# Expert rows stored as fp16 halves, a quarter of the experts transposed by the DMA crossbar, down matrices stored by partition

## The chip, the cores and the metric

One core of a Trainium2 chip runs the whole program. The metric is device time in microseconds (us) of one execution; lower is better. Engines are named as in the profile: PE (TensorE matmul), PEld (its weight loads), DVE (VectorE), ACT (ScalarE), POOL (GpSimd), SP (SyncE, which here only issues transfers).

## The reference

One post-layernorm decoder layer on x of 16 sequences x 256 rows x 512 columns (4096 rows in all), float32:

```python
x = layernorm(x + self_attention(x))          # 3 heads of width 512, averaged, then fc_w
x = layernorm(x + cross_attention(x, ctx))    # 16 heads of 32, causal
x = layernorm(x + ffn(x))
# ffn: router over 64 experts, top 6 of each row, at most 128 rows per expert
buf = rows of x gathered per expert                       # (64, 128, 512)
g = silu(einsum('ech,ehf->ecf', buf, w_gate))             # F = 352
u = einsum('ech,ehf->ecf', buf, w_up)
d = einsum('ecf,efh->ech', g * u, w_down)
y = sum over the row's 6 experts of weight * d
y = y + (silu(x @ sh_gate.T) * (x @ sh_up.T)) @ sh_down.T # shared expert, width 704
```

## The kernel before

Every matrix product is done in fp16 with each float32 operand split into a high half and a low half (x = high + low); three products high*high, high*low, low*high are summed (`PASSES`). Splitting takes one ACT copy (the high half) and one DVE subtraction (the low half).

The program has three stages. `prepare` folds weights (to about 71 us). `attend` loops over the 16 sequences in 18 software-pipelined bodies (to about 1290 us); it ends each sequence with the second layernorm's rows `x2`. `experts` runs the 64 experts, with jobs of the shared expert in between (to about 1940 us), and then normalizes and stores.

**End of a sequence in `attend`.** ACT (ZH, L1164) writes the high half of x2 to `x2r`, DVE (ZL, L1307) the low half. SP (L847) stores x2 as float32 rows to `x2_d` (for the gathers) and to `moe_d` (the sums), then waits for the halves and issues two crossbar transposes (L852) of `x2r` to `x2s`, each 128 x 1024 fp16, waits for them, and stores `x2s` to `x2T_d` (L855). The router's product on PE reads `x2s`.

**Experts.** `all_jobs` writes one list `MOE` of steps, and every engine walks it in this order, doing its own part. The steps of turn e are: G(e) gate product; HT(e-1) transposes of the hidden rows; U(e) up product; X(e+1) transposes of the next expert's gathered rows; WG(e+1) weight split; one to three jobs of the shared expert; WU(e+1); D(e-1) down product; WD(e). PE jobs use 8 PSUM banks in a ring. A step X(e) is four float32 128x128 transposes on PE (L1766) against an identity, with stride 4 through the row, so that chunk c holds columns 4q+c; then ACT (L1854) writes the high half and DVE (L1948) the low half of `xgs`. POOL gathers the rows of expert e (L1665, 128 rows of 2 KB) into one of three slots of `xg`; the slot is free once X(e-3) is done on PE. POOL also adds each expert's output to `moe_d` (L1680), one add at a time, in the order of the list.

**SP in the experts.** After each weight split is done on DVE (semaphore `w_low`), SP issues the load of the same matrix for expert e+3: L144 for gate or up (704 KB, one transfer, 5632 bytes per partition), L151 and L154 for down (512 and 192 KB, runs of 2 KB). All go through one hardware queue, as do the crossbar transposes.

## Time and profile before

| | |
|---|---|
| median of 3 runs | 2048.06 us (2028.49 to 2049.26) |
| the profiled execution's own time | 2014.67 us |
| its span, first to last instruction | 2012.9 us |
| granted TensorE clock, mean | 0.993 |
| PE busy | 1953.1 us (97%) |
| DVE, ACT, POOL busy | 1667.5, 1021.5, 692.8 us |
| DMA packets, MB | 202021, 285.59 |

The span is what the instructions cover; the time of the execution adds 1.8 us around it. The three timed runs lie 14 to 35 us above the profiled one. Busy shares are averages over stages: what bounds the kernel is read stage by stage. In a row of the timeline the first number is the start in us from the span's start and the second the duration; for queues (SPq) it is the time in which the instruction was issued, and the transfer's landing comes later.

### The profile page before, as it was taken

Reading aid. Unit: us, or ns where it says so; the run is one execution under the profiler, and the core shown is the slowest. Engines: PE = TensorE matmul, PEld = TensorE weight load, DVE = VectorE, ACT = ScalarE, POOL = GpSimd, SP = SyncE. Lnnn points to the kernel's source line nnn. Section 1 sums busy time; section 2 is a strip of 40 time slices with the busy share of each in tenths; the row PEclk is TensorE's granted clock in tenths of the full one; section 3 lists DMA queues with packets and bytes.
Section 4 is the critical chain, followed back from the end, with each engine's and each line's share of the span. In section 5 each row is a group of like instructions: output and inputs, shape, how many; then the busy total and the mean of one; then the engine's idle time right before and its main releaser. Section 6 shows DMA issues by size and latency. Waiting matters only on the chain.

```text
span 2012.9 us, 42821 instructions
## 1 busy us (share of the span) xinstructions
PE 1953.1 (97%) x16720; PEld 1204.0 (60%) x16720; DVE 1667.5 (83%) x3829; ACT 1021.5 (51%) x1553; POOL 692.8 (34%) x710
## 2 busy tenths in 40 slices
PE   8999999999999999999999987899999999999998
PEld 3656666676666666667666653355555555555553
DVE  5557988988998999998999888658888888888767
ACT  5424535444453554445355354445665656566545
POOL 1002232232232222223222322434565455554623
PEclk9999999999999999999999989999999999999999
DMA  6810121122122022112201233589999999999948
GB/s 230 75 42 22 57 77 43 38 76 54 36 67 77 23 57 77 45 45 67 77 23 57 67 113 91 154 240 281 309 291 289 302 284 305 299 282 307 292 84 322
DMA packets 202021, 285.59 MB, mean 142 GB/s; under 512 B 100283, under 2 KB 110523, under 8 KB 201820
## 3 DMA queue, kind: packets, MB, share of 16 engines
q1 hardware_dynamic: 177692, 242.85, 38.7%
q0 software_dynamic: 24128, 40.01, 10.3%
q8 instruction: 133, 2.18, 0.4%
q14 instruction: 68, 0.56, 0.1%
HBM read 208.67 MB, written 57.42 MB: 132 GB/s over the span
## 4 chain that ended last, share of the span: by engine, by line
PE 83%; DVE 11%; ACT 2%; issue 2%; DMA 1%; POOL 1%; SPq 0%; ACTq 0%; POOLq 0%; DVEq 0%
PE ring L932 33%; PE moe_bank L1731 27%; PE ring L992 6%; DVE quad L1314 5%; PE moe_bank L1800 5%; PE fold L485 3%; PE ring L1056 2%; PE quad L1039 2%; PE moe_bank L1766 1%; DVE maxima L1314 1%; PE ring L1064 1%; PE moe_bank L1778 1%; DVE x_rows_split L1307 1%; DMA slot_table<-table_records,slot_of_choice 1%; PE fold L469 1%
## 5 line engine op out<-in xcount | busy, mean ns | idle before, releaser
L178 POOL DMA_INDIRECT slot_table<-table_records,slot_of_choice x204 | 203.8, 999 | 420.6 <-PE ring L932 316.8
L932 PE MATMUL ring<-tion_then_expert_weights,xT_split 128*128 128x512 f16 x1152 | 264.8, 379 | 1.9 <-DVE scratch L1266 1.9
L932 PE MATMUL ring<-xT_split,tion_then_expert_weights 128*128 128x256 f16 x2304 | 264.6, 273 | 0.0
L932 PEld LDWEIGHTS ring<-xT_split,tion_then_expert_weights 128*128 128x128 f16 x2304 | 222.9, 98 | 36.5 <-issue 2.4
L1168 ACT ACTIVATE scratch<-ring 128x512 f16<-128x512 f32 x192 | 114.0, 594 | 215.8 <-PE ring L932 215.8
L1680 POOL DMA_INDIRECT expert_sums<-tion_then_expert_weights,scatter_index x64 | 121.8, 1903 | 190.9 <-PE moe_bank L1731 58.9
L932 PEld LDWEIGHTS ring<-tion_then_expert_weights,xT_split 128*128 128x128 f16 x1152 | 109.0, 98 | 126.1 <-issue 4.7
L1314 DVE CUSTOM_DVE_ANT_0 quad<-quad,causal_penalty 128x128 f32<-128x128 f32 (+1 forms) x512 | 165.7, 396 | 11.0 <-PE quad L1022 9.7
L1266 DVE SCALAR_TENSOR_TENSOR scratch<-ring,scratch 128x512 f16<-128x512 f32 x192 | 128.9, 685 | 21.2 <-ACT scratch L1168 21.1
L932 PE MATMUL ring<-scratch,xT_split 128*128 128x256 f16 x1152 | 138.8, 273 | 0.0
L902 POOL TENSOR_SCALAR_AFFINE_SELECT scratch<-scratch 128x1024 f32<-128x1024 f32 x64 | 70.5, 1104 | 193.5 <-ACT scratch L1188 170.9
L1731 PE MATMUL moe_bank<-w_down_split,hidden_T_split 128*128 128x512 f16 x576 | 134.8, 379 | 0.0
L992 PE MATMUL ring<-scratch,weights_split 128*128 128x512 f16 x576 | 129.5, 379 | 0.0
L1731 PE MATMUL moe_bank<-w_up_split,gathered_T_split 128*128 128x352 f16 x768 | 125.0, 312 | 2.9 <-DVE w_up_split L1951 1.7
L932 PEld LDWEIGHTS ring<-scratch,xT_split 128*128 128x128 f16 x1152 | 110.3, 98 | 24.9 <-issue 5.5
L1731 PE MATMUL moe_bank<-w_gate_split,gathered_T_split 128*128 128x352 f16 x768 | 125.0, 313 | 0.0
L1665 POOL DMA_INDIRECT gathered<-x_rows,gather_index x64 | 103.5, 1618 | 58.4 <-POOL gather_index L1653 16.7
L1330 DVE RECIPROCAL inv_denominator<-ring 128x256 f32<-128x256 f32 x64 | 112.1, 1751 | 12.7 <-PE ring L1064 12.6
L1324 DVE TENSOR_TENSOR scratch<-scratch 128x1536 f16<-128x1536 f32 x64 | 111.9, 1751 | 7.9 <-ACT scratch L1193 7.4
L1731 PE MATMUL moe_bank<-scratch,tion_then_expert_weights 128*128 128x512 f16 x528 | 118.4, 379 | 0.0
L1188 ACT ACTIVATE scratch<-quad 128x1536 f32<-128x1536 f32 x64 | 92.9, 1451 | 35.2 <-PE quad L1043 34.6
L1800 PE MATMUL moe_bank<-shared_down,scratch 128*128 128x512 f16 x480 | 108.8, 379 | 0.0
(248 smaller groups left out, 3962.5 us busy)
## 6 DMA issues: line engine op xcount, KB each, us to landing
gate_up_landing<-in_w_gate SPq DMA_DIRECT2D x43, 704.0 KB, 5.6
gate_up_landing<-in_w_up SPq DMA_DIRECT2D x43, 704.0 KB, 5.4
scratch<-in_w_down SPq DMA_DIRECT2D x43, 512.0 KB, 4.8
scratch<-in_w_gate SPq DMA_DIRECT2D x21, 704.0 KB, 5.5
scratch<-in_w_up SPq DMA_DIRECT2D x21, 704.0 KB, 5.9
tion_then_expert_weights<-in_w_down SPq DMA_DIRECT2D x21, 512.0 KB, 4.7
scratch<-in_w_down SPq DMA_DIRECT2D x43, 192.0 KB, 6.4
xT_in<-in_xT SPq DMA_DIRECT2D x16, 512.0 KB
```

The costliest lines, as they stand in the source:

```text
L178: pool.indirect_dma_start(self.dram, bass.IndirectOffsetOnAxis(ap=self.slot[:, tb, c:c + 1], axis=0), self.record[:, tb, c, :], None, boun ...
L932: last = pe.matmul(out_, left(a, c), right(b, c), start=(n == 0 and not onto), stop=(n == 3 * chunks - 1))
L992: last = pe.matmul(o[:, :], ws[:, a, j, t, g * P:(g + 1) * P], v[:, c, j, t, :], start=False, stop=(j, t, a) == (H - 1, NB - 1, 1))
L1168: act.activation(half(0), src, ACT.Copy, scale=scale).then_inc(high, 1)
L1266: dve.scalar_tensor_tensor(half(1), src, scale, half(0), ALU.mult, ALU.subtract)\
L1314: last = dve.tensor_tensor_reduce(out=quad[:, r, lo:lo + n], in0=quad[:, r, lo:lo + n], in1=w["causal"][:, N - n:N], scale=1.0, scalar=-3e ...
L1324: dve.tensor_tensor(ps[:, g % 2, 1, :, :], p32[:, g % 2, :, :], ps[:, g % 2, 0, :, :], ALU.subtract).then_inc(pready, 1)
L1330: link(dve.reciprocal(rden[:, :], o[:, N:2 * N]))
L1665: pool.indirect_dma_start(xg[:, s, :], None, x2_d, bass.IndirectOffsetOnAxis(ap=gi[:, s, :], axis=0), bounds_check=T + CAP - 1).then_inc(g ...
L1680: pool.indirect_dma_start(moe_d, bass.IndirectOffsetOnAxis(ap=si[:, s, :], axis=0), d32[:, s, :], None, bounds_check=T + CAP - 1, compute_ ...
L1731: last = pe.matmul(out_, left(a, c), right(b, c), start=(n == 0), stop=(n == 3 * chunks - 1))
L1800: pe.matmul(o[:, :], hs[:, s, a, f, b0:b0 + P], sd[:, b, f, :], start=(k == 0), stop=False)
```

## The change

1. `x2_d` holds each row as 1024 fp16 numbers (512 high halves, then 512 low halves), as wide in bytes as before. Within a half the columns are permuted: chunk c (128 numbers) holds columns 4q+c. ACT (ZH) and DVE (ZL) read x2 with a stride of 4 elements to write `x2r` so. The store to `x2_d` now reads `x2r` and stands behind the two transposes on SP's queue, ahead of its wait for them. The router's and the shared expert's weights (`gateT`, `sgT`, `suT`) are loaded with the same permutation.
2. For 48 experts, X(e) is eight fp16 128x128 transposes without a stride, and ACT and DVE copy the transposed halves out of PSUM. For the 16 experts 3, 7, ..., 63 the step is called XC: SP waits for the gather and for U(e-2) on PE, then issues one crossbar transpose of `xg` straight to `xgs`; PE, ACT and DVE do nothing. G(e) then waits for the landing (`crossed`), and so does POOL before it gathers expert e+3 into that slot. XC stands in the list where X stood.
3. `w_down` is rearranged on the host so that each partition's numbers lie together: the two loads (L151, L154) become one of 32 partitions x 4 KB and one of 96 partitions x 6 KB.

```diff
@@ Loads.down
-        to, w_down = self.wf["WD"][e % 3].rearrange("p (c n) -> p c n", c=FC), self.weights["WD"]
-        sp.dma_start(to[:, 0:FC - 1, :],
-                     w_down[e:e + 1, 0:(FC - 1) * P, :].rearrange("o (c p) n -> p (o c) n", p=P))\
+        to, w_down = self.wf["WD"][e % 3], self.weights["WD"]
+        two, p0 = (FC - 1) * E, FC * P - F
+        sp.dma_start(to[0:p0, 0:two], w_down[e:e + 1, 0:p0 * two].rearrange("o (p n) -> p (o n)", p=p0))\
           .then_inc(self.w_in["WD", e % 3], 16)
-        sp.dma_start(to[FC * P - F:P, FC - 1, :],
-                     w_down[e:e + 1, (FC - 1) * P:F, :].rearrange("o p n -> p (o n)"))\
+        sp.dma_start(to[p0:P, :], w_down[e:e + 1, p0 * two:F * E].rearrange("o (p n) -> p (o n)", p=P - p0))\
           .then_inc(self.w_in["WD", e % 3], 16)
...
@@ attend, on_sync
-                for d in (x2_d, moe_d):
-                    sp.dma_start(d[bass.ds((i - 2) * N, N), :].rearrange("(t p) e -> p t e", p=P),
-                                 x2[:, :, :]).then_inc(x2_stored, 16)
+                sp.dma_start(moe_d[bass.ds((i - 2) * N, N), :].rearrange("(t p) e -> p t e", p=P),
+                             x2[:, :, :]).then_inc(x2_stored, 16)
                 sp.wait_ge(x2T_stored, b.n(0, 0, 16, 1))
                 sp.wait_ge(x2_split, b.n(0, 0, 1, 1))
                 for t in range(NB):
                     sp.dma_start_transpose(x2s[:, t, :, :, :].rearrange("p a c n -> p (a c) n"),
                                            x2r[:, t, :, :].rearrange("p a e -> p (a e)")).then_inc(x2T_in, 16)
+                sp.dma_start(x2_d[bass.ds((i - 2) * N, N), :].rearrange("(t p) e -> p t e", p=P),
+                             x2r[:, :, :, :].rearrange("p t a e -> p t (a e)")).then_inc(x2_stored, 16)
                 sp.wait_ge(x2T_in, b.n(0, 0, 32, 32))
...
+    def by_chunk(rows):
+        return rows[:, :, :].rearrange("p t (q c) -> p t c q", c=EC)
...
@@ attend, on_scalar, ZH
-                    act.activation(x2r[:, :, 0, :], x2[:, :, :], ACT.Copy).then_inc(x2_high, 1)
+                    act.activation(x2r[:, :, 0, :].rearrange("p t (c q) -> p t c q", c=EC), by_chunk(x2),
+                                   ACT.Copy).then_inc(x2_high, 1)
@@ attend, on_vector, ZL
-                    dve.tensor_tensor(x2r[:, :, 1, :], x2[:, :, :], x2r[:, :, 0, :], ALU.subtract)\
-                       .then_inc(x2_split, 1)
+                    low, high_ = (x2r[:, :, a, :].rearrange("p t (c q) -> p t c q", c=EC) for a in (1, 0))
+                    dve.tensor_tensor(low, by_chunk(x2), high_, ALU.subtract).then_inc(x2_split, 1)
...
+CROSSED = [e for e in range(3, NX) if e % 4 == 3]
...
@@ all_jobs
-            order.append(("X", e + 1))
+            order.append(("XC" if e + 1 in CROSSED else "X", e + 1))
...
@@ experts, on_sync
+            elif step[0] == "XC":
+                e = step[1]
+                sp.wait_ge(gathered[e % AHEAD], 16 * (e // AHEAD + 1))
+                sp.wait_ge(full, MOE_JOBS["U", e - 2])
+                sp.dma_start_transpose(xgs[:, e % 2, :, :, :].rearrange("p a c n -> p (a c) n"), xg[:, e % AHEAD, :])\
+                  .then_inc(crossed, 16)
...
@@ experts, gather
-                pool.wait_ge(full, MOE_JOBS["X", e - AHEAD])
+                if e - AHEAD in CROSSED:
+                    pool.wait_ge(crossed, 16 * (CROSSED.index(e - AHEAD) + 1))
+                else:
+                    pool.wait_ge(full, MOE_JOBS["X", e - AHEAD])
...
@@ experts, on_tensor
-                for c in range(EC):
-
-                    last = pe.transpose(o[:, c * P:(c + 1) * P],
-                                        xg[:, e % AHEAD, :].rearrange("p (q c) -> p c q", c=EC)[:, c, :],
-                                        ident[:, :])
+                for k in range(2 * EC):
+                    last = pe.transpose(o[:, :].bitcast(F16)[:, k * P:(k + 1) * P],
+                                        xg[:, e % AHEAD, k * P:(k + 1) * P], ident16[:, :])
...
                 if name == "G":
-                    pe.wait_ge(free, MOE_FREED["X", e])
+                    if e in CROSSED:
+                        pe.wait_ge(crossed, 16 * (CROSSED.index(e) + 1))
+                    else:
+                        pe.wait_ge(free, MOE_FREED["X", e])
...
@@ experts, on_vector
+                if name == "X":
+                    dve.tensor_copy(half(1), bank_of(step)[:, :].bitcast(F16)[:, cols:2 * cols]).then_inc(free, 1)
+                    continue
                 dve.tensor_tensor(half(1), bank_of(step)[:, 0:cols], half(0), ALU.subtract).then_inc(free, 1)
```

## Rows read from the trace of the kernel before

**Rows 1.** Windows: us, busy of PE, PEld, DVE, ACT, POOL; PEclk, DMA share, GB/s

```profile
71.00:1195.00 1124.00, 1106.94 (x11816) 738.38 (x11814) 982.56 (x2920) 528.31 (x949) 295.58 (x291) 1.00 0.23 54
...
1400.00:1600.00 200.00, 199.42 (x1148) 115.88 (x1146) 166.15 (x170) 122.15 (x145) 105.61 (x88) 1.00 0.99 296
```

**Rows 2.** Waits of PE in the expert stage: total us, times, longest

```profile
PE moe_bank L1731 <- DVE w_up_split L1951: 1.7, 1, 1.7
PE moe_bank L1731 <- ACT silu_out L1867: 1.2, 4, 0.3
```

**Rows 3.** Chain that ended last, 1450 to 1460: start us, us, what

```profile
1454.38 0.33 PE moe_bank L1778 x3
...
1456.50 0.47 PE moe_bank L1766 x4
```

**Rows 4.** Groups of instructions, 1290 to 1940: busy us, mean ns, idle before

```profile
L1766 PEld LDWEIGHTS moe_bank<-ident,gathered 128*128 128x128 f32 x256 | 37.5, 203 | 3.3
...
L1778 PEld LDWEIGHTS moe_bank<-ident,hidden 128*128 128x128 f32 x189 | 24.6, 141 | 3.8
```

**Rows 5.** Timeline of PE in the attention loop

```profile
1007.88 0.28 PE L1027 MATMUL ring<-ident,maxima 128*128 128x128 f16 x2
1007.99 0.86 PE L932 MATMUL ring<-gate_split,scratch 128*128 128x64 f16 x24
```

**Rows 6.** Timeline of SP's queue, ahead of experts 3, 7 and 59

```profile
1348.77 0.38 SPq L151 DMA_DIRECT2D tion_then_expert_weights<-in_w_down  x1
1349.19 0.47 SPq L154 DMA_DIRECT2D tion_then_expert_weights<-in_w_down  x1
...
1385.54 0.47 SPq L154 DMA_DIRECT2D scratch<-in_w_down  x1
...
1892.47 0.47 SPq L154 DMA_DIRECT2D scratch<-in_w_down  x1
```

**Rows 7.** Timeline of PE, gate products of experts 3, 7 and 59

```profile
1354.47 1.95 PE L1731 MATMUL moe_bank<-w_gate_split,gathered_T_split 128*128 128x352 f16 x12
...
1393.78 1.51 PE L1731 MATMUL moe_bank<-w_gate_split,gathered_T_split 128*128 128x352 f16 x9
...
1896.82 1.36 PE L1731 MATMUL moe_bank<-w_gate_split,gathered_T_split 128*128 128x352 f16 x8
```

**Rows 8.** DMA issues, 1290 to 1940: KB each, median us to landing

```profile
gate_up_landing<-in_w_gate SPq DMA_DIRECT2D x41, 704.0 KB, 5.6
```

**Rows 9.** Line 154, second down transfer: issues and their landing

```profile
DMA to landing us min/median/max: 4.0/6.6/11.1
```

**Rows 10.** Timeline of SP's queue, crossings behind other transfers

```profile
1202.49 0.50 SPq L847 DMA_DIRECT2D expert_sums<-scratch  x1
1204.46 5.72 SPq L852 DMA_TRANSPOSE scratch<-x_rows_split  x2
1213.92 0.36 SPq L855 DMA_DIRECT2D x_transposed<-scratch  x1
```

**Rows 11.** DMA issues, 1202 to 1216: median us to landing

```profile
expert_sums<-scratch SPq DMA_DIRECT2D x1, 512.0 KB, 7.8
```

**Rows 12.** Line 852, crossings of x2: issues and their landing

```profile
DMA to landing us min/median/max: 3.1/3.2/7.1
```

**Rows 13.** Windows, crossings alone on the queues (columns as Rows 1)

```profile
1210.00:1212.00 2.00, 2.00 (x17) 0.90 (x10) 2.00 (x12) 0.39 (x1) 0.23 (x1) 1.00 1.02 206
```

**Rows 14.** Chain at the end of the attention loop

```profile
1261.83 1.07 ACT x_rows_split L1164
...
1262.92 1.24 DVE x_rows_split L1307
...
1265.61 3.92 DMA scratch<-x_rows_split
```

**Rows 15.** Waits of POOL and DVE, 1290 to 1940

```profile
POOL expert_sums L1680 <- PE moe_bank L1731: 58.9, 17, 7.6
...
DVE tion_then_expert_weights L1976 <- DMA expert_sums<-tion_then_expert_weights,scatter_index: 1.6, 2, 0.9
```

More of the change, by code:

```diff
@@ L263, in build @@
         with ExitStack() as s:
-            moe = experts(nc, Memory(nc, s), ident, loads, table, x2_d, x2T_d, table_d, moe_d, out,
+            moe = experts(nc, Memory(nc, s), ident, ident16, loads, table, x2_d, x2T_d, table_d, moe_d, out,
                           layers.signals)
@@ L1532, with experts @@
 MOE_ADDS = places(s for s in MOE if s[0] == "D" or s[0] == "SD" and s[1] < LATE_DOWN and s[2] % 2)
-MOE_GATHERS = places([("X", 0), ("X", 1)] + [("X", s[1] + 2) for s in MOE if s[0] == "X" and s[1] + 2 < NX])
 MOE_FREED = places(s for s in MOE if s[0] in ("X", "HT", "D") or s[0] == "SD" and s[1] < LATE_DOWN)
-def experts(nc, mem, ident, loads, table, x2_d, x2T_d, table_d, moe_d, out, layers):
+def experts(nc, mem, ident, ident16, loads, table, x2_d, x2T_d, table_d, moe_d, out, layers):
     gu = loads.gate_up
@@ L1700, in on_gpsimd @@
         for step in MOE:
-            if step[0] == "X" and step[1] + AHEAD < NX:
+            if step[0] in ("X", "XC") and step[1] + AHEAD < NX:
                 gather(step[1] + AHEAD)
@@ L2008 @@
     flat = np.asarray(x).reshape(T, E)
+    down, p0 = np.asarray(L0_ffn_w_down), FC * P - F
+    chunks = down[:, 0:(FC - 1) * P, :].reshape(NX, FC - 1, P, E).transpose(0, 2, 1, 3)
+    three = np.concatenate([chunks[:, p0:], down[:, (FC - 1) * P:, :].reshape(NX, P - p0, 1, E)], axis=2)
+    by_partition = np.concatenate([chunks[:, 0:p0].reshape(NX, -1), three.reshape(NX, -1)], axis=1)
     arrays = {
```

24 lines of the change are left out of this document (13 added, 11 removed).

## The prediction

> **What bounds the kernel now.** I read the windows first, to see which stage has which limit. In the expert stage PE is busy 199.4 of 200 us at full granted clock, and DMA shows a share of 0.99 with 296 GB/s; in the attention loop PE is busy 1107 of 1124 us and DMA only 0.23 [rows 1]. So PE sets the pace in both, and DMA is the resource with nothing to spare beside it in the experts. The waits of PE confirm it: in 615 us of experts it lost 2.9 us to other engines, and not once to a transfer [rows 2]. A faster DVE, ACT or POOL therefore gives nothing; only PE work taken off the path, or a new wait of PE, moves the end.
>
> **The transposes on PE.** In the chain an X step takes 0.47 us for four float32 transposes [rows 3]. The three unstrided float32 transposes of HT take 0.33 us, 0.11 each against 0.12: the stride shows in the weight loads (203 against 141 ns [rows 4]) but hardly in the pace. An fp16 128x128 product against an identity takes 0.055 us: two of them fill the 0.11 us before the next group starts [rows 5]. Eight make 0.44 us. So the 48 experts that stay on PE gain 48 x 0.03 = 1.4 us (between a loss of 4 us, if each of the eight cost 0.07, and that gain), and the 16 crossed experts gain 16 x 0.47 = 7.5 us. What ACT and DVE save lies beside PE and counts nothing. The crossed step also leaves the ring of PSUM banks, so each bank comes round one job later in time; the only bank waits are the 2.9 us named, so nothing either way.
>
> **The crossing and its deadline.** This is the step that decides. XC(e) stands on SP behind WD(e-2), so SP comes to it right after it has issued the two down transfers for expert e+1. For expert 3 they are issued at 1348.77 and 1349.19, and SP is free at 1349.66 [rows 6]. PE starts G(3) at 1354.47 [rows 7]: 4.8 us later. For expert 7, with two shared jobs in the turn, it is 1386.01 to 1393.78, 7.8 us; for expert 59 it is 1892.94 to 1896.82, 3.9 us. Rows 6 and 7 hold the first, the widest and the last of 15 such pairs (expert 63 has no down transfer ahead of it); their mean is 4.85 us, 13 of them lie between 3.9 and 5.2, one is 6.2. The times in SP's queue follow PE, because DVE's down split waits behind the scaling of D(e-3) that PE has just finished; a PE that waits at G(e) does not move SP's next XC earlier relative to it. And since X(e) itself is gone from PE, PE is at G(e) 0.47 us sooner: 4.4 us are there.
>
> What is needed: a crossing alone lands 3.2 us after its issue starts [rows 12]. That would fit. But it is in one queue behind 704 KB of down weights. Today's second down piece lands 6.6 us (median; 4.0 to 11.1) after its issue [rows 9], which is 6.1 us after the XC would be issued. The changed down load has 128 long runs like the gate load, which is as large and lands in 5.6 us [rows 8]; counted from the first down issue, 0.9 us before XC, that is 4.7 us after it. On top comes the crossing's own time behind a busy queue. The trace has one such case: a store issued at 1202.49 landed after 7.8 us, at 1210.3 [rows 11], two crossings issued behind it from 1204.46 on, and SP went on at 1213.92, when both were in [rows 10]; 3.6 us for two, 1.8 for one. While they moved, the core's DMA made 206 GB/s [rows 13], so 256 KB need 1.3 us of it. Crossing landed at 4.7 + 1.8 = 6.5 us after its issue, against 4.4 us there. Over the 15 pairs max(0, 6.5 + 0.47 - slack) sums to 32.6 us (two turns with wide slack lose 0.8 and 0). The same sum is 0 if it lands after 3.2 us, 12 at 5.0, 40 at 7.0, and 80 at 9.7 (6.1 and both crossings' 3.6). I take 6.5, nearest to the two rows of like size and like neighbours, and keep 0 and 80.
>
> The Trainium skill (Advanced Engine Details and Errata, X-Bar Transpose) says that transposing transfers run as fast as regular ones, at 350 to 400 GB/s. By it 256 KB would need about 0.7 us, an estimate from that page, and the stalls would shrink by some 0.6 us each, 9 us in all. The row with 206 GB/s speaks against it, though with other stores waiting on their landing it is no clean measurement.
>
> **What the crossing's wait holds up elsewhere.** SP itself waits for nothing new: the gather of a crossed expert was called for three turns before, and U(e-2) is done. Each XC costs SP 1.3 us of issue, covered by its waits. The next weight loads queue behind it, but they are for three experts ahead, and a turn takes some 10 us. POOL's gather of e+3 waits for the landing instead of PE's X(e), up to 6 us later than now in the tight turns, and the add of D(e-2) stands behind it. POOL waits 58.9 us for PE's results in all, and DVE waited for an add twice, 1.6 us [rows 15]; so about 1 us per expert is free there, and the added delay is spread over four turns and partly matched by PE's own stall. I cost it at 0, and at 30 us if that cover is gone.
>
> **Down loads by partition.** 352 runs of 2 KB become 128 of 4 or 6 KB. No one waits for the loads [rows 2], so it is worth nothing by itself; its part is in the 4.7 us above (6.1 without it). Permuted loads of the shared and router weights happen once, early, beside PE: 0.
>
> **The end of a sequence.** ZH and ZL now read with a stride of 16 bytes. Both are on the chain once, in the last body, at 1.07 and 1.24 us [rows 14]. The nearest price of such a stride is the weight load, 203 against 141 ns, a factor of 1.44: +0.5 and +0.5, 1.0 us in the last body. In the 15 earlier bodies PE covers them (DVE is 87% busy there [rows 1]); I allow 1 us, with ends of 0 and 15 x 0.5 = 8. The Trainium skill (SBUF — State Buffer, Door 1) says that the memory has lines of 16 bytes and that a read which finds a new line at each access pays for it; this is a rule against the change, and by it the two instructions lengthen, by how much it does not say. If they don't, 2 us fall away. The store moved behind the crossings frees their way: in the last body they landed in 3.9 us against 3.2 alone [rows 12, 14], -0.7 us. Its own issue fits in SP's wait for them.
>
> **Sum.** +32.6 - 7.5 - 1.4 + 2.0 - 0.7 = +25 us: 2014.7 becomes 2039.7 in the profiled execution. The timed runs before have a median 33 us above it, so +25 on the median: 2073 us. A change under 1% (20 us) can't be told from none.
>
> **Rivals.**
> *The crossing lands in time.* If the queue's transfers overlap instead of following one another, it lands within 4.4 us and all that remains is -7.5 - 1.4 + 1.3: -8 us, 2040. For it: the fastest down piece landed in 4.0 us, and 3.2 us suffice alone. Against it: the 3.6 us behind a busy queue, and a DMA share of 0.99. This is the side on which my forecast is wrong in sign.
> *The adds become the bound.* POOL's chain of gather and add is behind by the crossing's landing every fourth turn; if it can't catch up, DVE waits for `added` in D(e), and PE behind it. +30 on top of the forecast, or the long landings of 7.9 us, sum 53: +45 to +60, 2100. It decides from a landing of about 8 us on. For it: the loaded DMA; against it: 58.9 us of slack.
> *The stride costs DVE in every body.* +8 instead of +1 with the rest as forecast: 2080. PE's 98% in the loop speaks against.
> *A real gain,* over 20 us: PE's busy time would have to shrink by more than its transposes; only if the lighter down loads sped up more than the profile shows. Nothing in the rows speaks for it.
>
> **Chances.** Forecast, stalls of 1 to 3 us per crossed expert (+8 to +45): 0.5, of which 0.3 lies beyond +20. Crossing in time: 0.27, within 1%. Adds or long landings: 0.1; stride: 0.05; both slower. A gain: 0.08. So faster 0.08, within 1% 0.47, slower 0.45. The forecast's own range is 2056 to 2093. The range asked for reaches down to the crossing in time with the scatter of the median (2034) and up to a landing of 8 us (2106).
>
> **What would show it.** In the profile after: PE's wait list gets a wait of the gate product for a transfer from `gathered` to `gathered_T_split`, about 15 times, about 2 us each; none if the first rival holds. The landing of that transfer is the number to read: 6.5 forecast, under 4.4 for the rival. The X group on PE has 384 instructions at a pace of 0.055 us. POOL's gathers e+3 start later after crossed experts; DVE waits for adds stay under 5 us. ZH and ZL in the last body near 1.5 and 1.8 us. The expert stage's windows keep PE at 1.00 clock. The prediction fails if the crossings overtake the down data, or if SP comes to XC at another point than behind WD(e-2).

## The result and the profile after

The changed kernel is slower, by 3.4%:

| | before | after |
|---|---|---|
| median of 4 runs each | 2038.28 us (2018.68 to 2049.26) | 2101.06 us (2093.65 to 2108.12) |
| ratio | | 1.0341, 95% interval 1.0236 to 1.0445 |
| the profiled execution's own time | 2014.67 us | 2100.53 us |
| span | 2012.9 us | 2098.5 us |
| granted TensorE clock, mean | 0.993 | 0.977 |
| PE busy | 1953.1 us | 1970.1 us |

The forecast had said +25 us; it is +63 on the medians and +85.6 on the spans. The range held the time, the size of the change was missed. PE is busy 17.0 us longer although its transposes should have cost 8.9 us less, and idle 68.6 us longer (85.6 - 17.0). The profiled execution before is faster than all four timed ones, so the spans differ by more than the medians.

**Windows of the kernel after** (columns as in [rows 1]):

```profile
71.00:1195.00 1124.00, 1102.18 (x11785) 735.21 (x11783) 984.09 (x2898) 537.45 (x938) 293.88 (x290) 1.00 0.22 54
1400.00:1600.00 200.00, 187.11 (x1090) 105.56 (x1089) 143.39 (x150) 108.07 (x127) 99.34 (x78) 0.97 0.98 274
1600.00:1800.00 200.00, 175.66 (x994) 97.14 (x991) 132.16 (x139) 101.14 (x118) 94.06 (x73) 0.93 0.98 256
```

Where PE was busy 199.4 of 200 us [rows 1] it is now busy 187 and then 176, and the granted clock, 1.00 before, is 0.97 and 0.93. The loss is mainly in the expert stage: the first gate product starts at 1335.81 instead of 1324.93, 10.9 us late, and the other 74.7 us come behind it.

**Waits of PE, 1322 to 2010, and the landing of the crossings (line 1642), kernel after:**

```profile
PE moe_bank L1746 <- DMA gathered_T_split<-gathered: 57.1, 14, 8.1
PE moe_bank L1746 <- DVE w_up_split L1971: 2.1, 2, 1.7
```

```profile
  PE moe_bank L1746: 57.1, 14
  POOL expert_sums L1695: 11.6, 2
busy tenths in 40 slices 0000000000000000000000000000000000000000
DMA to landing us min/median/max: 5.0/7.5/13.8
```

The first row is new against [rows 2]: 14 waits of 4.1 us in the mean, 57.1 us. The forecast had about 2 us each; the landing is 7.5 us (median) where it had 6.5, and the largest is 13.8.

**One crossing in the timelines of SP's queue and of PE, kernel after:**

```profile
1437.72 0.33 SPq L152 DMA_DIRECT2D scratch<-in_w_down  x1
1438.09 0.45 SPq L154 DMA_DIRECT2D scratch<-in_w_down  x1
1438.64 1.63 SPq L1642 DMA_TRANSPOSE gathered_T_split<-gathered  x1
1440.31 0.58 SPq L144 DMA_DIRECT2D scratch<-in_w_gate  x1
```

```profile
1441.02 2.10 PE L1746 MATMUL moe_bank<-w_down_split,hidden_T_split 128*128 128x512 f16 x9
1445.42 3.29 PE L1746 MATMUL moe_bank<-w_gate_split,gathered_T_split 128*128 128x352 f16 x12 [2.30 <-DMA gathered_T_split<-gathered]
...
1663.78 3.68 PE L1746 MATMUL moe_bank<-w_gate_split,gathered_T_split 128*128 128x352 f16 x12 [5.76 <-DMA gathered_T_split<-gathered]
```

The crossing is issued 0.92 us after the first down transfer, as the forecast had it. PE is through with the work before G(e) at 1443.12, 4.5 us later, and waits 2.30 us. Then the gate product of 12 matmuls takes 3.29 us, and 3.68 behind a wait of 5.76, instead of the 1.95 us of [rows 7]. All 12 products at the lower of the clock's two levels (1.2 instead of 2.4 GHz) would be 3.9 us, and the granted clock around the second of them is 0.53:

```profile
1663.00:1668.00 5.00, 4.22 (x17) 2.52 (x18) 0.00 (x0) 0.46 (x1) 1.48 (x3) 0.53 0.98 325
```

A stall thus costs its own length and up to 1.7 us more behind it. Of the 15 gate products behind such a stall 12 took 2.45 to 3.68 us, and three, behind stalls of 0.77, 0.99 and 2.07 us, took 1.95. **All 768 gate matmuls together, before and after:**

```profile
L1731 PE MATMUL moe_bank<-w_gate_split,gathered_T_split 128*128 128x352 f16 x768 | 125.0, 313 | 0.0
L1746 PE MATMUL moe_bank<-w_gate_split,gathered_T_split 128*128 128x352 f16 x768 | 141.8, 340 | 58.1 <-DMA gathered_T_split<-gathered 57.1
```

**End of the attention loop: instructions of lines 1169 and 1314 (ZH, ZL), kernel after,** duration in ns min/median/max, first and last start in us:

```profile
L1169 ACT ACTIVATE x_rows_split<-scratch x16: 2012/2076/2082, 208.3 to 1269.5; 128x1024 f16<-128x1024 f32 x16
```

```profile
L1314 DVE TENSOR_TENSOR x_rows_split<-scratch,x_rows_split x16: 1973/1998/2007, 210.9 to 1271.6; 128x1024 f16<-128x1024 f32 x16
```

In the last body they had taken 1.07 and 1.24 us [rows 14]; now 2.01 and 1.97. The last ZH starts at 1269.5 instead of 1261.83, 7.7 us late.

### The profile page after: what moved, and what is told of

Same layout as the page of the kernel before. It is cut to its first block, busy times and chain, and to the rows that moved or that the text cites. A ratio compares the mean times of both kernels' runs of the same rounds, so it can differ in the third digit from the quotient of the medians.

```text
span 2098.5 us, 43061 instructions
## 1 busy us (share of the span) xinstructions
PE 1970.1 (94%) x16848; PEld 1201.6 (57%) x16848; DVE 1655.6 (79%) x3813; ACT 1030.7 (49%) x1537; POOL 706.9 (34%) x710
## 4 chain that ended last, share of the span: by engine, by line
PE 68%; DVE 14%; DMA 9%; issue 4%; ACT 3%; POOL 1%; SPq 1%; ACTq 0%; POOLq 0%; DVEq 0%
PE ring L933 31%; PE moe_bank L1746 17%; PE ring L993 6%; DMA gathered_T_split<-gathered 6%; DVE quad L1320 5%; PE moe_bank L1816 3%; PE fold L485 2%; PE ring L1057 2%; PE quad L1040 2%; DVE w_down_split L1971 1%; DVE maxima L1320 1%; PE ring L1065 1%; DVE w_up_split L1971 1%; PE moe_bank L1780 1%; DVE x_rows_split L1314 1%
## 5 line engine op out<-in xcount | busy, mean ns | idle before, releaser
L933 PEld LDWEIGHTS ring<-xT_split,tion_then_expert_weights 128*128 128x128 f16 x2304 | 222.7, 98 | 36.6 <-issue 2.4
L1746 PE MATMUL moe_bank<-w_gate_split,gathered_T_split 128*128 128x352 f16 x768 | 141.8, 340 | 58.1 <-DMA gathered_T_split<-gathered 57.1
L1695 POOL DMA_INDIRECT expert_sums<-tion_then_expert_weights,scatter_index x64 | 128.3, 2005 | 188.7 <-DMA expert_sums<-tion_then_expert_weights,scatter_index 59.7
L1746 PEld LDWEIGHTS moe_bank<-w_gate_split,gathered_T_split 128*128 128x128 f16 x768 | 79.0, 104 | 118.2 <-issue 60.8
L1884 ACT ACTIVATE silu_out<-moe_bank 128x352 f32<-128x352 f32 x64 | 29.6, 462 | 191.9 <-PE moe_bank L1746 191.9
L1680 POOL DMA_INDIRECT gathered<-x_rows,gather_index x64 | 96.2, 1503 | 58.4 <-POOL gather_index L1665 34.2
```

The lines of the kernel that those rows point to most:

```text
L933: last = pe.matmul(out_, left(a, c), right(b, c), start=(n == 0 and not onto), stop=(n == 3 * chunks - 1))
L1680: pool.indirect_dma_start(xg[:, s, :], None, x2_d, bass.IndirectOffsetOnAxis(ap=gi[:, s, :], axis=0), bounds_check=T + CAP - 1).then_inc(g ...
L1695: pool.indirect_dma_start(moe_d, bass.IndirectOffsetOnAxis(ap=si[:, s, :], axis=0), d32[:, s, :], None, bounds_check=T + CAP - 1, compute_ ...
L1746: last = pe.matmul(out_, left(a, c), right(b, c), start=(n == 0), stop=(n == 3 * chunks - 1))
```

## The experiments

The kernels ran in five batches, each on one chip together with runs of the kernel before. The median of the kernel before differs between batches (2019 to 2075 us; on one chip 2025 in batch 4 and 2075 in batch 5), so kernels of different batches are compared by their ratio to it alone; a point is a hundredth of its time. In the profiles of batches 2 and 5 the first gate product starts at 1370 to 1382 us, in all others at 1322 to 1337, so start times are not laid side by side across these batches.

| kernel | batch | median us | ratio | 95% interval |
|---|---|---|---|---|
| all_on_pe | 1 | 2073.0 | 1.024 | 1.016 to 1.032 |
| no_stride | 1 | 2088.25 | 1.036 | 1.028 to 1.044 |
| cross_unused | 1 | 2092.98 | 1.037 | 1.031 to 1.044 |
| cross_early | 1 | 2092.46 | 1.036 | 1.031 to 1.042 |
| down_only | 2 | 2107.02 | 1.021 | 1.016 to 1.025 |
| rows_old_down | 2 | 2068.4 | 1.001 | 0.997 to 1.006 |
| cross_old_down | 2 | 2124.33 | 1.029 | 1.025 to 1.033 |
| early_best | 2 | 2096.75 | 1.017 | 1.012 to 1.021 |
| before_three | 3 | 2013.95 | 0.997 | 0.994 to 1.001 |
| down_three | 3 | 2047.58 | 1.013 | 1.007 to 1.019 |
| after_three | 3 | 2100.87 | 1.040 | 1.034 to 1.046 |
| best_three | 3 | 2041.19 | 1.010 | 1.007 to 1.014 |
| down_again | 4 | 2061.26 | 1.020 | 1.014 to 1.026 |
| down_cut | 4 | 2035.93 | 1.006 | 1.002 to 1.009 |
| halves | 4 | 2023.06 | 0.999 | 0.995 to 1.003 |
| rows_old_three | 4 | 2014.59 | 0.997 | 0.993 to 1.000 |
| down_split_first | 5 | 2111.16 | 1.015 | 1.009 to 1.021 |
| before_split_first | 5 | 2090.03 | 1.007 | 1.004 to 1.011 |

### Batch 1: is it the crossing?

**all_on_pe.** The kernel after with every X on PE.

```diff
-CROSSED = [e for e in range(3, NX) if e % 4 == 3]
+CROSSED = []
```

> The changed kernel with no expert crossed: all 64 take the eight fp16 transposes on PE. Queue theory (the loss is PE waiting for a crossing that stands in the queue behind the down weights, and the half clock after the wait): the 57 us of waits and some 18 us of clock are gone, 7 us of PE work come back: 2100.6 - 75 + 7 = about 2030 us, ratio to the kernel before 1.00 to 1.01 (what stays is the strided splits, 10 us, less 3). Rival (the fp16 rows, the eight transposes or the new down loads cost the time in the experts): it stays above 2050, ratio over 1.02.

It came out at 1.024. With no crossing at all, but with the stride, 2.4% are lost, so the crossing is at most a part of it, and the expectation of 1.00 to 1.01 was a miss. **Its waits of DVE and of PE, 1322 to 1990:**

```profile
DVE tion_then_expert_weights L1996 <- DMA expert_sums<-tion_then_expert_weights,scatter_index: 95.6, 33, 9.5
```

```profile
PE moe_bank L1746 <- DVE hidden_T_split L1968: 33.0, 8, 6.0
```

DVE waits 95.6 us for adds into `moe_d`, where it was 1.6 us [rows 15], and PE waits for DVE. This is the forecast's second rival, without the crossing that was to bring it about.

**no_stride.** ZH and ZL write plain halves, and the permutation goes to the host for the weights that meet these rows.

```diff
-act.activation(x2r[:, :, 0, :].rearrange("p t (c q) -> p t c q", c=EC), by_chunk(x2), ACT.Copy)
+act.activation(x2r[:, :, 0, :], x2[:, :, :], ACT.Copy)
...
-dve.tensor_tensor(low, by_chunk(x2), high_, ALU.subtract)
+dve.tensor_tensor(x2r[:, :, 1, :], x2[:, :, :], x2r[:, :, 0, :], ALU.subtract)
...
-"w_gate": rows(L0_ffn_w_gate), "w_up": rows(L0_ffn_w_up)   # so too gateT, sgT, suT
+"w_gate": partitions(L0_ffn_w_gate), "w_up": partitions(L0_ffn_w_up)
```

> The changed kernel with ZH and ZL unstrided again (the columns are put in chunk order on the host, in the weights, instead). Stride theory: ACT 2072 to 1045 ns, DVE 1998 to 1216 ns, 0.5 us per body of the attention loop and 2 us at its end: 10 us less than the changed kernel, about 2091 us, ratio to before about 1.029; the wait of PE for crossings unchanged at about 57 us. Rival (the 7.5 us in the loop are another effect, such as the moved store): ZH and ZL get shorter but the time stays at 2101.

ZH is back at 1045 ns, the last one starts at 1260.3 instead of 1269.5, and the first gate product at 1324.5 instead of 1335.8. So the stride cost about 11 us ahead of the experts, all of the delay found there. The timed ratio, 1.036, cannot be told from that of the kernel after: PE still waits 53.4 us for crossings and DVE 12.3 us for adds.

**cross_unused.** All X on PE, and 16 crossings that nobody reads, into a spare buffer.

```diff
+spare = mem.sb("spare_T", [P, 2 * EC, P], F16)
-sp.dma_start_transpose(xgs[:, e % 2, :, :, :].rearrange("p a c n -> p (a c) n"), xg[:, e % AHEAD, :])
+sp.dma_start_transpose(spare[:, :, :], xg[:, e % AHEAD, :])
```

> The changed kernel with all 64 experts transposed on PE, and the 16 crossings issued as well, at the same place, into a buffer that nothing reads; POOL still waits for them before it reuses the slot. Queue theory: only the wait of PE matters, so the time is that of the kernel with all on PE within 5 us, about 2030 to 2035. Rival (the crossing's traffic slows the weight loads, gathers and adds, and these slow PE): well above it, 2060 or more, with PE waiting for weights or DVE for adds.

1.037, where all_on_pe has 1.024, and PE waits for no crossing: crossings that nobody reads cost 1.3 points (each interval reaches 0.6 to 0.8 to either side), as the waits show, through the adds. POOL still waits for them, 12.3 us in all; what that does and what the traffic does is not told apart. DVE waits 124.4 us for adds, 41 times, and PE 44.5 us for DVE.

**cross_early.** XC(e) is issued right behind the gate load, ahead of SP's wait for the split of the up weights: at 1429.81 for a gate product that starts at 1439.67, 9.9 us ahead, where it was 4.5.

```diff
+if step[0] == "WU" and step[1] + 1 in CROSSED:
+    cross(step[1] + 1)
...
-elif step[0] == "XC":
```

> The changed kernel with each crossing issued about 7 us sooner: on SP right after the gate load that follows WG(e-1) and before the wait for WU(e-1), so ahead of up and down loads instead of behind them. Queue theory: it lands 6 to 8 us after issue, before PE is at G(e); the waits of PE fall from 57 us to under 10, the clock stays at 1.00, and the time is 7 us under the kernel with all on PE: about 2023 us, ratio 0.995 to 1.005. Rival (a crossing is slow wherever it stands, 10 us and more in this traffic): waits of 30 us and more remain, 2060.

**Waits of PE and of DVE in cross_early, 1322 to 1990:**

```profile
PE moe_bank L1749 <- DVE hidden_T_split L1971: 45.2, 10, 6.4
...
PE moe_bank L1749 <- DMA gathered_T_split<-gathered: 2.8, 2, 1.7
```

```profile
DVE tion_then_expert_weights L1999 <- DMA expert_sums<-tion_then_expert_weights,scatter_index: 150.8, 45, 9.5
```

The wait for crossings is gone, 2.8 us instead of 57.1, and the time did not move (1.036). DVE's waits for adds rose from 6.5 us to 150.8. A turn is held up by whichever chain is later; with the crossing's wait taken away, the adds were next.

### Batch 2: the down loads

**down_only.** The kernel before with the down loads by partition and nothing else.

```diff
-sp.dma_start(to[:, 0:FC - 1, :], w_down[e:e + 1, 0:(FC - 1) * P, :].rearrange("o (c p) n -> p (o c) n", p=P))
+sp.dma_start(to[0:p0, 0:two], w_down[e:e + 1, 0:p0 * two].rearrange("o (p n) -> p (o n)", p=p0))
...
-sp.dma_start(to[FC * P - F:P, FC - 1, :], w_down[e:e + 1, (FC - 1) * P:F, :].rearrange("o p n -> p (o n)"))
+sp.dma_start(to[p0:P, :], w_down[e:e + 1, p0 * two:F * E].rearrange("o (p n) -> p (o n)", p=P - p0))
```

> The kernel before with only the down matrices by partition (runs of 4 and 6 KB). The run with all experts on PE was 46 us slower than before, with DVE waiting 96 us for adds to moe_d (1.6 before) and the adds landing after 8.3 us (7.2 before). Add theory (longer runs in SP's queue take the DMA engines from POOL's 2 KB rows, the adds land later, and their chain becomes the bound): 25 to 40 us slower than before, ratio 1.012 to 1.02, DVE waiting over 50 us for adds. Rival (the fp16 rows, or DVE's fp16 copies beside POOL, slow the adds; the down runs do nothing): ratio 0.995 to 1.005, adds at 7.2 us.

1.021: the part that the forecast put at nothing costs 2.1% alone. DVE waits 81.6 us for adds (1322 to 1990).

**rows_old_down.** The other half: fp16 rows, all transposes on PE, no stride (the edit of no_stride), and the down loads of the kernel before.

```diff
-CROSSED = [e for e in range(3, NX) if e % 4 == 3]
+CROSSED = []
...
-"w_down": rows(by_partition)
+"w_down": rows(L0_ffn_w_down)
```

> fp16 rows, all experts on PE, no strided splits, down matrices as before (2 KB runs): what is left of the change is the fp16 rows and the eight transposes. Add theory: ratio 0.993 to 1.003, adds at 7.2 us, DVE waiting under 10 us for them. Rival (fp16 rows and copies): 1.012 to 1.02, adds at 8 us.

1.001: the fp16 rows cost nothing and bring nothing that can be measured. But DVE waits 36.6 us for adds, 14 times, where under 10 us were expected.

**cross_old_down.** The kernel after with the down loads of before.

```diff
-sp.dma_start(to[0:p0, 0:two], w_down[e:e + 1, 0:p0 * two].rearrange("o (p n) -> p (o n)", p=p0))
+sp.dma_start(to[:, 0:FC - 1, :], w_down[e:e + 1, 0:(FC - 1) * P, :].rearrange("o (c p) n -> p (o c) n", p=P))
```

> The changed kernel with only the down loads as before. Add theory: the adds are no bound in the changed kernel itself (DVE waited 6.5 us for them), since PE's waits for crossings give them time, so little changes: PE still waits 50 to 65 us for crossings, 2090 to 2105 us, ratio 1.025 to 1.04. If the wait for crossings also comes from the long runs ahead of them, it falls under 40 us and the time to 2070.

1.029, with 35.2 us of PE's waits for crossings, 12 times. **The landing of its crossings (line 1643):**

```profile
DMA to landing us min/median/max: 4.5/6.4/12.4
```

Behind the old down loads the crossings land sooner (6.4 against 7.5 us) and PE waits less (35.2 against 57.1 us); the two profiles are of different batches. The time followed at most in part (1.029 against 1.034, with overlapping intervals); 2070 us was expected for this case. So crossing with stride costs 2.9% alone and the down loads 2.1% alone, yet both together 3.4%: the two do not add.

**early_best.** The early crossing, no stride (as in no_stride), the down loads of before.

```diff
+if step[0] == "WU" and step[1] + 1 in CROSSED:
+    cross(step[1] + 1)
...
-"w_down": rows(by_partition)
+"w_down": rows(L0_ffn_w_down)
```

> Crossings issued early (behind the gate load), no strided splits, down loads as before: what should be the best form of the idea. Add theory: adds at 7.3 us, no waits of PE for crossings, PE work 9 us less than before: ratio 0.994 to 1.0. Rival (the crossings' own traffic delays the adds, as the run with unused crossings, 14 us over the run without, suggests): adds at 7.7 us and more, DVE waiting 50 us for them, ratio 1.01 to 1.02.

1.017: the crossing at its best still loses, with 73.1 us of DVE's waits for adds and 6.6 us of PE's for crossings.

### Batch 3: a third buffer for the scaled expert output

DVE's D(e) scales the down product into one of two buffers and so waits for the add of e-2. With three it waits for that of e-3.

```diff
-if e >= 2:
-    dve.wait_ge(added, 16 * MOE_ADDS["D", e - 2])
-dve.tensor_scalar(d32[:, e % 2, :], bank_of(step)[:, :], ...)
+if e >= 3:
+    dve.wait_ge(added, 16 * MOE_ADDS["D", e - 3])
+dve.tensor_scalar(d32[e % 3], bank_of(step)[:, :], ...)
```

It was put into the kernel before (before_three), down_only (down_three), the kernel after (after_three) and early_best (best_three).

> The kernel before with a third buffer for the scaled expert outputs: DVE's D(e) waits for the add of expert e-3 instead of e-2. In the slow runs so far 34 to 37 of some 60 adds take POOL 3.1 us to issue instead of 1.6, nearly all of them while DVE runs the down split: DVE's scaling and POOL's next add are released by the same landing, so DVE's long instruction meets POOL's. Coupling theory: three buffers part the two; adds at 3.1 us become rare, DVE waits under 10 us for adds, ratio 0.985 to 1.0. Rival (the 3.1 us come from DMA traffic alone): no change in their count, ratio 1.00.

> The kernel before with the down matrices by partition (1.021 alone) and the third buffer. Coupling theory: the longer runs only tip the adds into the coupled state; with three buffers most of the 2.1% comes back, ratio under 1.005. Rate theory (the longer runs take DMA time from the adds, and the chain of adds is too slow whatever the buffers): ratio stays 1.015 to 1.025 with DVE waiting over 50 us.

> The changed kernel with the third buffer. Its own adds are hardly late (DVE waits 6.5 us), since PE's waits for crossings give them time; both theories: ratio 1.028 to 1.038, PE waits 50 to 60 us for crossings.

> Early crossings, no strided splits, down loads as before (1.0165) and the third buffer. Coupling theory: ratio 0.98 to 0.995, DVE waits for adds under 15 us, PE's work 9 us less than before. Rate theory: 1.01 to 1.02.

With the buffer the kernel with the new down loads stands at 1.013 instead of 1.020 to 1.021, early_best at 1.010 instead of 1.017, the kernel before at 0.997, and the kernel after, whose waits are for crossings, at 1.040. Each interval reaches 0.4 to 0.6 to either side. Against before_three the down loads still cost 1.6 points, so by this pair the third buffer takes back 0.4 points of their price, no more than the scatter. The coupling theory of the expectations had under 1.005 for down_three and 0.98 to 0.995 for best_three, and missed both. In down_three 16 adds take POOL 2.8 us or more to issue (8 in before_three); DVE's waits for adds are 28.5 us, and 20.0 us of PE's waits for gathered rows stand in their place: gathers and adds are issued by the same POOL, one after the other.

### Batches 4 and 5: why the loads slow the adds

**down_again** is down_only once more, beside its variants.

> The kernel before with the down loads by partition and nothing else, on the chip of the two that follow, so that they can be laid beside it. Every theory expects a ratio of about 1.021, as down_only had, and adds that land some 8.3 us after issue.

**POOL and DVE in down_again, two turns of the timeline, 1600 to 1660** (start us, duration us):

```profile
1625.35 0.75 DVE L1975 TENSOR_SCALAR tion_then_expert_weights<-moe_bank,records 128x512 f32<-128x512 f32 x1 [1.37 <-DMA expert_sums<-tion_then_expert_weights,scatter_index]
1626.01 1.75 DVE L1950 SCALAR_TENSOR_TENSOR w_down_split<-scratch,w_down_split 128x1536 f16<-128x1536 f32 x1
1626.09 3.15 POOL L1679 DMA_INDIRECT expert_sums<-tion_then_expert_weights,scatter_index  x1 [3.68 <-DMA expert_sums<-tion_then_expert_weights,scatter_index]
...
1634.30 0.75 DVE L1975 TENSOR_SCALAR tion_then_expert_weights<-moe_bank,records 128x512 f32<-128x512 f32 x1 [1.38 <-DMA expert_sums<-tion_then_expert_weights,scatter_index]
1634.96 1.75 DVE L1950 SCALAR_TENSOR_TENSOR w_down_split<-tion_then_expert_weights,w_down_split 128x1536 f16<-128x1536 f32 x1
1635.04 3.15 POOL L1679 DMA_INDIRECT expert_sums<-tion_then_expert_weights,scatter_index  x1 [0.96 <-PE moe_bank L1777]
```

**The same two steps in the kernel before:**

```profile
1616.61 0.74 DVE L1976 TENSOR_SCALAR tion_then_expert_weights<-moe_bank,records 128x512 f32<-128x512 f32 x1
1617.27 1.75 DVE L1951 SCALAR_TENSOR_TENSOR w_down_split<-scratch,w_down_split 128x1536 f16<-128x1536 f32 x1
1619.94 1.61 POOL L1680 DMA_INDIRECT expert_sums<-tion_then_expert_weights,scatter_index  x1 [0.89 <-PE moe_bank L1766]
```

Here is the loop. In these rows of before, DVE scales and splits without a wait, and POOL issues the next add later, by itself, in 1.61 us. In down_again DVE waits for an add; when it lands, DVE scales, begins its 1.75 us down split, and 0.08 us later POOL begins the next add. Behind the start of that split the issue takes 3.15 us instead of 1.6. So the add lands 1.5 us later, DVE waits for it again, and the next turn begins the same way. The Trainium skill (SBUF — State Buffer, "SBUF: two separate sides") describes such a trap: a transfer issued from GpSimd has its descriptors written by that engine, over ports that DVE can hold. The rows agree as to the effect, 3.15 against 1.61 us; the page names copies and other 2-port modes for it, and here it is a scalar_tensor_tensor with two operands.

Which of the two begins first decides. **Two more adds of the kernel before, 1830 to 1844, each with DVE's down split:**

```profile
1831.79 1.75 DVE L1951 SCALAR_TENSOR_TENSOR w_down_split<-scratch,w_down_split 128x1536 f16<-128x1536 f32 x1
1831.87 3.15 POOL L1680 DMA_INDIRECT expert_sums<-tion_then_expert_weights,scatter_index  x1 [4.37 <-PE moe_bank L1731]
...
1840.84 1.61 POOL L1680 DMA_INDIRECT expert_sums<-tion_then_expert_weights,scatter_index  x1 [2.99 <-PE moe_bank L1731]
1840.98 1.75 DVE L1951 SCALAR_TENSOR_TENSOR w_down_split<-tion_then_expert_weights,w_down_split 128x1536 f16<-128x1536 f32 x1
```

An add issued 0.08 us behind the split's start takes 3.15 us, one issued 0.14 us ahead of it 1.61. In both kernels an add that begins clearly inside a split takes what is left of the split and some 1.5 us more: 2.73 us when it begins 0.54 us into the down split (at 1444.15, before), 2.94 us when it begins 0.17 us into the gate split of 1.63 us (at 1602.65). Adds that begin 0.07 us or more ahead of one take 1.6 to 1.7 us, unless another split was running already.

**Groups of POOL's adds, 1330 to 1950, in down_again and in down_cut** (before it was 63 at a mean of 1908 ns):

```profile
L1679 POOL DMA_INDIRECT expert_sums<-tion_then_expert_weights,scatter_index x56 | 151.9, 2712 | 181.9 <-PE moe_bank L1730 61.6 <-DMA expert_sums<-tion_then_expert_weights,scatter_index 46.1 <-DMA expert_sums<-tion_then_expert_weights 27.8
```

```profile
L1681 POOL DMA_INDIRECT expert_sums<-tion_then_expert_weights,scatter_index x60 | 126.9, 2115 | 195.2 <-DMA expert_sums<-tion_then_expert_weights,scatter_index 58.3 <-PE moe_bank L1732 50.1 <-DMA expert_sums<-tion_then_expert_weights 43.2
```

**The chain of waits in down_again, 1600 to 1660, by line:**

```profile
by line: DMA expert_sums<-tion_then_expert_weights,scatter_index 92.7%; issue 7.8%; PE moe_bank L1730 2.0%; POOLq L186 0.8%; POOLq L1679 0.3%
```

In this stretch the chain is not PE's but that of the adds, 93% of it, one every 8 to 10 us. I took each indirect add's landing and POOL's issue of it from the trace, for all adds of 1330 to 1961, as means:

| | adds | issue us | landing us | landing less issue | issues of 2.8 us or more |
|---|---|---|---|---|---|
| before | 64 | 1.9 | 6.8 | 4.9 | 9 |
| halves | 63 | 2.0 | 6.8 | 4.8 | 12 |
| down_cut | 61 | 2.1 | 7.3 | 5.2 | 13 |
| down_again | 57 | 2.7 | 8.0 | 5.3 | 38 |
| all_on_pe | 57 | 2.6 | 7.9 | 5.3 | 36 |
| cross_early | 56 | 2.7 | 8.3 | 5.5 | 40 |
| after | 56 | 2.0 | 7.8 | 5.7 | 12 |

Of the 1.2 us by which an add lands later in down_again, 0.4 is the transfer and 0.8 is POOL's longer issue. (The expectations name 7.2 and 8.3 us for these landings; by the means of this table it is 6.8 and 8.0.)

**down_cut.** The same layout in five pieces with runs of 2 KB.

```diff
+for c in range(FC - 1):
+    sp.dma_start(to[0:p0, c * E:(c + 1) * E], low[:, c * E:(c + 1) * E]).then_inc(self.w_in["WD", e % 3], 16)
+for c in range(FC):
+    sp.dma_start(to[p0:P, c * E:(c + 1) * E], high[:, c * E:(c + 1) * E]).then_inc(self.w_in["WD", e % 3], 16)
```

> As down_again, but each down load is cut into pieces whose runs are 2 KB long, where down_again has runs of 4 and 6 KB. If it is the length of the runs in SP's queue that lets the adds into moe_d land late (8.3 us in down_only, 7.2 before), they land near 7.2 us again and the ratio is near 1.00 (up to 1.007). If it is the layout by partition itself, in which part of the transfer touches 96 partitions, or its landing, the adds stay near 8.3 us and the ratio near 1.02. More issues on SP could cost up to 0.2% by themselves (3 more of them a body at 0.08 us, all under SP's waits).

1.006 beside 1.020 for down_again: shorter runs in the same layout take back 1.4 of the 2.0 points, and DVE's waits for adds fall from 112.6 us to 32.6. The length of the runs is the cause of the larger part; it is not the size of one transfer, since the kernel before has one of 512 KB in runs of 2 KB. What the other 0.6% are, the layout or five issues in place of two, is not told apart.

**halves.** The kernel before with gate and up loads in two parts, runs of 2.8 KB instead of 5.6.

```diff
+for k in range(2):
+    sp.dma_start(self.wf[name][e % 3][:, k * half:(k + 1) * half], src[:, k * half:(k + 1) * half])
```

> The kernel before with each gate and up load cut in two along the free axis: runs of 2.8 KB instead of 5.6 KB, nothing else. If long runs slow the adds, these were slow already in the kernel before: adds land under 7.2 us, and the ratio is 0.99 to 1.00. If the length of runs plays no part, 1.00 with adds at 7.2 us. If more and smaller packets load the queue, 1.00 to 1.01.

0.999: the long runs that were there before cost nothing that can be measured. So it is no rule that long runs are bad by themselves. In the kernel before they alternated with down transfers of 2 KB runs and the adds were just in time; whether the alternation is what counts wasn't tried.

**rows_old_three.** rows_old_down with the third buffer; the edits are those shown above.

```diff
-CROSSED = [e for e in range(3, NX) if e % 4 == 3]
+CROSSED = []
...
+dve.tensor_scalar(d32[e % 3], bank_of(step)[:, :], ...)
```

> The half of the change that cost nothing (rows stored as fp16 halves, all transposes on TensorE, ZH and ZL in two plain halves, down loads as before: 1.001 in rows_old_down) and a third buffer for the scaled expert output, with which DVE no longer waits for adds (0.997 for before_three). If TensorE's 17 us of shorter transposes were given back through DVE's waits for adds (36.6 us in rows_old_down), they come out now: 0.99. If POOL's one queue of gathers and adds holds them back, PE waits for gathered rows instead, and it is 0.995 to 1.00.

0.997 (0.993 to 1.000). It and before_three are the fastest kernels here; neither interval lies clear of 1.

**down_split_first and before_split_first.** WD(e) stands ahead of D(e-1) in the list, in down_only and in the kernel before.

```diff
-if e > 0:
-    order.append(("D", e - 1))
 if 0 < e < NX - 1:
     order.append(("WD", e))
+if e > 0:
+    order.append(("D", e - 1))
```

> down_only with one more edit: DVE (and ACT) do the down weight split WD(e) ahead of D(e-1) in the list, so that DVE has no 1.75 us split left to do at the moment at which an add lands and POOL writes the next. In down_again 38 of 57 indirect adds took POOL over 2.8 us to issue, each beside that split, and landed after 8.5 us in the mean; the 17 short ones landed after 7.0. If the loop between DVE's wait for an add and POOL's long issue is what multiplies the cost, long issues become rare (under 15), DVE's waits for adds fall from 112.6 us to under 30, and the ratio is 1.00 to 1.01. If the later landing behind long runs is enough by itself, DVE still waits 60 to 100 us, and the ratio stays at 1.015 to 1.02.

> The kernel before with the same reordering alone. Its DVE hardly waits for adds (1.6 us) and it has 9 long issues, so both theories expect 0.995 to 1.00. If the split ahead of D(e-1) keeps a PSUM bank or the scaled output busy 1.7 us longer and PE or POOL wait for it, it is 1.00 to 1.01, with a new wait of PE for DVE.

The long issues are gone as expected: of 59 adds 3 took 2.8 us or more, where down_again has 38 of 57. But DVE still waits 71.8 us for adds, where under 30 were expected, and the reordering costs 0.7% by itself, with 22.9 us of such waits (1340 to 2010 in both); 0.995 to 1.00 was expected. Against that (1.015 to 1.007) the loads cost 0.8 points instead of 2.0. The third buffer, which also breaks most of the long issues, left 1.6 points. Each of these differences carries some 0.6 to 0.7 points of scatter. So the loop is shown, row by row, and it is a part of the price; how large a part is not settled (1.2 points by one test, 0.4 by the other). Later landings hold DVE up without the loop too.

## Why the prediction was wrong

It was right that the kernel gets slower and that PE would wait for crossings; the change costs 3.4% and the forecast had 1.2. On the profiled pair the terms can be laid side by side, and they close to within 1 us of the 85.6:

| us | forecast | measured |
|---|---|---|
| PE's waits for crossings | +32.6 | +57.1 |
| PE's busy time from the first gate product on | -8.9 | +16.8 |
| delay of the first gate product | +1.3 | +10.9 |
| sum | +25.0 | +84.8 |

Step by step:

- **The down loads by partition: "No one waits for the loads [...] so it is worth nothing by itself; its part is in the 4.7 us above (6.1 without it)." This is the step that failed, in both halves.** By itself the new layout costs 2.1% (down_only) and 2.0% (down_again). It was asked who waits for these loads, and not who shares the DMA engines with them. Nobody waits for them, but with them the add lands 1.2 us later, and [rows 15] had shown that DVE's margin for adds was thin: it had already waited for one twice. And the layout was counted on to bring the down data in 4.7 us after the crossing's issue. In the kernel after, its second piece is in after 6.0 us (median of 16; mean 6.5), and the crossing lands behind it; with the old loads the crossings landed sooner, not later (6.4 against 7.5 us). In the kernel after it is this second half that shows. Without this step the forecast would still have been short: with the old down loads (cross_old_down) the change costs 2.9%.
- **Crossing's landing, 6.5 us: mis-sized.** 7.5 us median, 8.1 in the mean, 5.0 to 13.8. The crossing's own part was 1.0 us behind the second down piece (median; mean 1.6) where 1.8 was taken; what is over comes from the 4.7. The mechanism and the issue points were as worked out (0.92 us behind the first down transfer, 4.5 us ahead of G in the example), 14 waits where 15 were counted. The sum that gave 32.6 us for 6.5 and 40 for 7.0 was 57.1; by the same working 7.5 gives 47 (15 pairs at 0.5 us more than for 7.0), and the late ones, up to 13.8 us, the rest.
- **"The expert stage's windows keep PE at 1.00 clock": wrong.** 0.97 and 0.93. PE is busy 17.0 us longer in all where 8.9 less were expected; those 25.9 us were in no term. The gate products behind the stalls account for 16.8 us (141.8 against 125.0), the up products and the hidden transposes that follow them for 3.7 and 3.3 more; the instructions are the same, and where they are slow the granted clock is near its lower level (0.53 over 1663 to 1668). What remains, 2 us, is not followed up.
- **The stride: mis-sized.** 2.0 us were allowed, and it cost about 11 (first gate product at 1335.8 after, 1324.5 in no_stride, 1324.9 before). ZH went from 1045 to 2076 ns and ZL from 1216 to 1998, factors of 2.0 and 1.6 where 1.44 was taken from the weight loads, and they are not covered in the loop: the last ZH starts at 1261.8 us before, at 1269.5 after and at 1260.3 in no_stride. The Trainium skill's rule that a read which finds a new line of 16 bytes at each access pays for it (SBUF — State Buffer, Door 1) is borne out by these rows; the forecast had named it and priced the stride too low. In the timed ratio no_stride does not show the gain.
- **Eight fp16 transposes, -1.4 us, and the 16 X off PE, -7.5:** the pace is right. From one product to the next an X takes 0.44 to 0.45 us. What the eight transposes save isn't seen in rows_old_down (1.001). Of the gain of the crossed ones nothing is left in any kernel that crosses.
- **The adds.** The rival "The adds become the bound" had the right chain but the wrong cause, late crossings. The adds bound the kernel with no crossing at all (all_on_pe), and in the kernel after DVE waits for them only 6.5 us, because PE's stalls at G give POOL time. In place of "58.9 us of slack" one should read the period of the chain: an issue of 1.9 us, a landing 4.9 us behind it, and then the next, in a turn of some 10 us that also holds gathers and the shared expert's adds.
- **The crossing lands in time (2040 us), the rival with a gain:** cross_early comes close to it (2.8 us of waits for crossings), and it was 1.036; with the old down loads and no stride (early_best) it was 1.017. What was missed is that such a kernel waits for adds instead.

The prices don't add. The waits fit a simple reading, that a stall from one chain is slack for the other: DVE waits 95.6 us for adds in all_on_pe and 6.5 in the kernel after, where PE waits 57.1 for crossings. Alone the loads cost 2.1% and the crossing with its stride 2.9%, together 3.4. On top of the down loads the crossing is worth 1.0 points (1.024 to 1.034); on top of the crossing the down loads are worth 0.5 (1.029 to 1.034), both from different batches and within their intervals' reach of each other.

Open stay: why the adds land 0.4 us later beside long runs (the runs show that they do, not how), how large the loop's share is, what makes some crossings land after up to 13.8 us, and whether the loop could be broken without the 0.7% of the reordering.

## What to carry to other kernels

When a transfer for which nobody waits is changed, list the transfers that share the DMA engines with it and look up the margin of each: the tightest one here was an add whose late landing had twice been waited for. A chain of one transfer at a time, each behind the last one's landing, is bounded by its period and not by its engine's idle time; and removing one wait proves nothing until the profile shows which wait took its place.

## What the runs showed of the hardware

- An indirect add takes POOL 1.6 us to issue, and 3.15 us when DVE's 1.75 us float32-to-fp16 split with two operands began 0.08 us ahead of it; begun 0.14 us behind the issue's start, the split left it at 1.61 us (both in the kernel before).
- Down loads with runs of 4 and 6 KB instead of 2 KB, of the same bytes, let adds from another queue land 0.4 us later (5.3 instead of 4.9 us behind the end of their issue); loads of 2.8 instead of 5.6 KB for gate and up changed nothing.
- A read with a step of 16 bytes made ACT's copy of 128 x 1024 2.0 times as long and DVE's subtraction 1.6 times.
- Behind a stall of PE of 2.3 us, 12 matmuls took 3.29 us instead of 1.95, behind one of 5.76 us 3.68; behind stalls of 0.77, 0.99 and 2.07 us they took 1.95. Around the slow ones the granted clock was 0.53 (1663 to 1668).
- A crossing of 256 KB behind 704 KB of down loads landed 7.5 us after its issue (median; 5.0 to 13.8) in the kernel after, and 6.4 us (4.5 to 12.4) behind down loads in 2 KB runs, in another batch (cross_old_down).
